# Soft-MoE expert outputs of a two-layer vision tower: stored from ScalarE's DMA queue instead of SyncE's, and read back in two sets

## What is computed

```python
xn = l2norm(x); phin = scale * l2norm(phi)
logits = einsum('bmd,dnp->bmnp', xn, phin)
d = softmax(logits, axis=1)                     # dispatch: over the tokens of an image
c = softmax(logits over n)                      # combine: over the 64 experts
xs = einsum('bmd,bmnp->bnpd', xn, d)            # one row for each image and expert
h = gelu(einsum('bnpd,ndh->bnph', xs, w1) + b1)
ys = einsum('bnph,nhd->bnpd', h, w2) + b2
y = einsum('bnpd,bmnp->bmd', ys, c)
```

## Time and profile before

| what | value |
|---|---|
| median of three runs | 980.36 us (977.6 to 984.06) |
| profiled execution, its own time | 982.76 us |
| its span, first to last instruction | 980.9 us |
| busy: TensorE, VectorE, ScalarE, GpSimd | 858.5, 455.5, 318.1, 280.1 us |
| experts stage with its combine | about 262 to 476 us of the span |
| bytes moved by DMA in all | 128.93 MB |

### The profile page before, as it was taken

How to read it: one execution, slowest core, us unless ns; L and a number is a source line. 1 busy time by engine, 2 the same in 40 slices (tenths; PEclk the granted TensorE clock), 3 DMA queues, 4 the chain that set the end, 5 groups by cost and what they waited for, 6 DMA issues and landing times. The chain is left out here.

```text
span 980.9 us, 17879 instructions
## 1 busy us (share of the span) xinstructions
PE 858.5 (88%) x6209; PEld 621.5 (63%) x6209; DVE 455.5 (46%) x1520; ACT 318.1 (32%) x904; POOL 280.1 (29%) x242
## 2 busy tenths in 40 slices
PE   6899999899999999893997999977465999999991
PEld 6787888676466655463854777757453666666661
DVE  6864565548443322241654688836781222222220
ACT  2544333237433332240042566633101121221210
POOL 1540000000000000000233455530027488888444
PEclk9999999799899999996997899985556999999996
DMA  8992000270089999982500000002005354455222
GB/s 265 281 329 97 2 2 2 81 305 2 23 320 423 423 422 423 425 263 70 175 1 1 1 2 0 1 2 53 24 24 140 79 105 104 92 101 104 39 24 25
DMA packets 59881, 128.93 MB, mean 131 GB/s; under 512 B 26334, under 2 KB 42256, under 8 KB 50112
## 3 DMA queue, kind: packets, MB, share of 16 engines
q1 hardware_dynamic: 29858, 118.61, 33.3%
q0 software_dynamic: 29952, 9.36, 7.0%
HBM read 115.76 MB, written 11.49 MB: 130 GB/s over the span
## 5 line engine op out<-in xcount | busy, mean ns | idle before, releaser
L1831 POOL DMA_INDIRECT out_dram<-yr,put x48 | 105.7, 2203 | 58.3 <-issue 35.4
L1286 POOL MEMSET xg<- 96x74 f32 x1 | 0.2, 157 | 406.9 <-PE bank L1259 406.9
L1818 POOL DMA_INDIRECT zr<-z_rows,take x48 | 66.6, 1388 | 84.6 <-issue 84.6
L1895 PE MATMUL bank<-zTa,w 128*128 128x372 f32 x256 | 90.0, 496 | 0.8 <-DVE zTb L1969 0.8
L1978 DVE TENSOR_TENSOR hT<-sg,bank 128x372 f32<-128x372 f32 x64 | 31.8, 538 | 107.5 <-ACT sg L1939 63.1
L1895 PEld LDWEIGHTS bank<-zTa,w 128*128 128x128 f32 x256 | 47.5, 194 | 38.2 <-ACT sg L1939 8.4
L1143 DVE COPY eh<-bank 128x384 f32<-128x384 f32 x32 | 17.8, 558 | 110.6 <-PE bank L1181 110.6
L1909 PE MATMUL bank<-w2r,hT 128*124 128x192 f32 x384 | 66.1, 329 | 0.8 <-DVE hT L1978 0.8
L1939 ACT ACTIVATE sg<-bank 128x372 f32<-128x372 f32 x64 | 27.3, 478 | 115.4 <-PE bank L1900 115.4
L1909 PEld LDWEIGHTS bank<-w2r,hT 128*124 128x124 f32 x384 | 61.9, 187 | 3.8 <-issue 3.8
L1327 POOL TENSOR_TENSOR nl<-nl,nr 111x1036 f32<-111x1036 f32 x22 | 42.1, 1914 | 61.7 <-DVE nr L1437 61.7
(11 more groups left out here) (298 smaller groups left out, 1798.4 us busy)
## 6 DMA issues: line engine op xcount, KB each, us to landing
w1l<-in_w_dram SPq DMA_DIRECT2D x20, 1152.0 KB, 16.3
w2l<-in_w_dram SPq DMA_DIRECT2D x20, 1152.0 KB, 16.9
w1s<-in_w_dram SPq DMA_DIRECT2D x12, 1152.0 KB, 15.5
w2s<-in_w_dram SPq DMA_DIRECT2D x12, 1152.0 KB, 15.1
w<-in_w_dram SPq DMA_DIRECT2D x8, 1024.0 KB, 8.0
xt<-in_x_dram SPq DMA_DIRECT2D x22, 336.0 KB, 8.0
xT<-in_xT_dram SPq DMA_DIRECT2D x22, 333.0 KB, 7.4
w2r<-in_w2r_dram SPq DMA_DIRECT2D x8, 384.0 KB, 4.1
```

The source lines that it names most:

```text
L1818: nc.gpsimd.indirect_dma_start(zr[b][:, j, :], None, z_rows, bass.IndirectOffsetOnAxis(ap=take[:, k:k + 1], axis=0), bounds_check=NROW - 1 ...
L1831: nc.gpsimd.indirect_dma_start(rows_out, bass.IndirectOffsetOnAxis(ap=put[:, k:k + 1], axis=0), yr[e % 2][:, j, :], None, bounds_check=OUT ...
L1895: nc.tensor.matmul(bank[to + 2 * part + half][:, 0:HS], w13[b][:, 0, at:at + 128], zTa[b][:, half * HS:(half + 1) * HS], start=True, stop= ...
```

## The change

The stores move from SP's loop into ScalarE's: right behind the copy of a pair's outputs, ScalarE waits for that copy to be complete and issues the two stores from its own DMA queue. All 32 pairs are stored to `ys`; the direct transfers and `places` are gone. SP's loop then holds weight loads alone; behind the last it waits for output of pair 27, loads b2, waits for the stores of pairs 24 to 27, and reads pairs 0 to 27 back in six transfers of 28 partitions; then it waits for the stores of pairs 28 to 31 and reads these back in six transfers of four partitions. TensorE's wait at the products is for b2 and the twelve read-backs alone.

```diff
-DIRECT = 27
+FIRST = 27
 def experts_sp(sp):
-    for s in range(NPAIR + RING):
+    for s in range(NPAIR):
         q = s % RING
...
         if s >= RING:
             sp.wait_ge(s_dy, s - RING + 1)
         sp.dma_start(w2s[q][:], ins["w2"][s]).then_inc(s_w2[q], 16)
-        p = s - RING
-        if p >= 0:
-            b = p % EOB
-            sp.wait_ge(s_do, p + 1)
...
-        if p == DIRECT:
+        if s == NPAIR - 1:
+            sp.wait_ge(s_dy, FIRST + 1)
             sp.dma_start(e2[NE:2 * NE, 0:T], ins["b2"].rearrange("n (t d) -> n t d", d=ED)).then_inc(s_el, 16)
...
+    for first, last in ((0, FIRST), (FIRST + 1, NPAIR - 1)):
+        for p in range(last + 1 - EOB, last + 1):
+            sp.wait_ge(s_eoo[p % EOB], rows_out_by(p))
+        for k in range(2):
+            read_back(sp, slice(k * NPAIR + first, k * NPAIR + last + 1))
+
+def read_back(sp, n):
+    for g in range(2):
+        to = slice(g * NE + n.start, g * NE + n.stop)
+        sp.dma_start(e1[to, 0:T - 1], ys_of[n, g * (T - 1):(g + 1) * (T - 1)]).then_inc(s_el, 16)
+    sp.dma_start(e2[n, 0:T], ys_of[n, 2 * (T - 1):B]).then_inc(s_el, 16)
...
     def output(p):
...
         nc.scalar.copy(eo[p % EOB][:], bank[6 + b][:, 0:ED]).then_inc(s_do, 1)
+        act.wait_ge(s_do, p + 1)
+        for e in range(2):
+            act.dma_start(ys_of[p + e * NPAIR], eo[p % EOB][e * B:(e + 1) * B]).then_inc(s_eoo[p % EOB], 16)
...
-    pe.wait_ge(s_el, 16 * (1 + 2 * GB))
-    for b in range(EOB):
-        pe.wait_ge(s_eoo[b], rows_out_by(NPAIR - EOB + b))
+    pe.wait_ge(s_el, 16 * (1 + 4 * GB))
```

More of the change, by code:

```diff
@@ L1059, in experts_sp @@
         def experts_sp(sp):
-            for s in range(NPAIR + RING):
+            for s in range(NPAIR):
                 q = s % RING
[L1062 to L1070, removed]
-                p = s - RING
-                if p >= 0:
-                    b = p % EOB
-                    sp.wait_ge(s_do, p + 1)
[L1075 to L1081, removed]
-                if p == DIRECT:
-                    sp.dma_start(e2[NE:2 * NE, 0:T], ins["b2"].rearrange("n (t d) -> n t d", d=ED)).then_inc(s_el, 16)
[L1084 to L1092, removed]
@@ L1094, in places @@
-        def places(n):
-            return ((e1[n:n + 1, 0:T - 1], 0, T - 1), (e1[NE + n:NE + n + 1, 0:T - 1], T - 1, 2 * (T - 1)), (e2[n:n + 1, 0:T], 2 * (T - 1), B))
+                if s == EARLY:
+                    sp.wait_ge(s_h, 2 * T)
+                if s >= RING:
+                    sp.wait_ge(s_dh, s - RING + 1)
+                sp.dma_start(w1s[q][:], ins["w1"][s]).then_inc(s_w1[q], 16)
+                if s >= RING:
+                    sp.wait_ge(s_dy, s - RING + 1)
+                sp.dma_start(w2s[q][:], ins["w2"][s]).then_inc(s_w2[q], 16)
@@ L1097, in rows_out_by @@
+        def read_back(sp, n):
[3 more added lines that the diff above has]
+            sp.dma_start(e2[n, 0:T], ys_of[n, 2 * (T - 1):B]).then_inc(s_el, 16)
         def rows_out_by(p):
-            return sum(16 * (2 if r < DIRECT else 2 * GB) for r in range(p % EOB, p + 1, EOB))
+            return 32 * (p // EOB + 1)
         def experts_act(act):
```

## The result

The changed kernel takes 987.16 us in the median of 20 runs (984.31 to 993.95), the kernel before 984.42 us in 20 runs beside it (977.6 to 987.67). The ratio is 1.0042, with a 95% interval of 1.0025 to 1.0058: 2.7 us or 0.25 to 0.58% slower, inside the 1% of no change and inside the range forecast; the forecast was 3.0 us slower. The profiled execution took 986.35 us (before 982.76).

What follows compares the result with a forecast made beforehand. Weights set the pace late in the experts stage, then the products wait for read-backs: 446.5 + 2.8 + 12.2 = 461.5 us against 458.53, 3.0 later, so 985.8 us profiled, 983.4 median; own range 979 to 987, wider range 973 to 991.

Steps and rivals of the forecast that it cites:

- T: Time when TensorE's first product after the experts can start: 458.53 us before the change, 461.5 forecast.
- Earlier weights: SP's weight loads in the experts stage, no longer behind store waits: net 0.6 us earlier, bounds 2.1 earlier and 0.5 later.
- Stores on ScalarE: Waits and two store issues a pair on ScalarE: 1.3 us a pair, hidden under its 2.52 us of idling.
- Rival C: ScalarE becomes the bound as its issues wait for SP's: 10 us slower, with the tail 994 us; chance 0.09.
- First set right behind b2, issued before 431: Read-back of pairs 0 to 27 follows b2, which ends at 431.2 us; takes 15.1 us, to 446.3.
- rival D: Stores wait behind all that is queued; first set starts no earlier than 434.3 us; 986.3 to 988.7 us; chance 0.15.
- When it can start: Second read-back set waits for pair 31's stores, which land with the first set's end, 446.5 us.
- Second set: Read-back of pairs 28 to 31, 0.39 MB in six four-partition transfers: 2.8 us issue and landing plus 12.2 us.
- slow end: Second read-back's six four-partition transfers one after another at 27 GB/s: 14.6 us.
- Sum: First product at 446.5 + 2.8 + 12.2 = 461.5 us, 3.0 later than 458.53; profiled execution 985.8, median 983.4.
- Rival A: The last stores land early, by 440.2 us; first product at 456.6 to 459.0, time 979.6 us; chance 0.25.
- B: Few partitions cost nothing: second read-back takes 2.2 us, first product 11.3 us earlier, time 969.1 us; chance 0.08.

Runs made afterwards that it cites:

- one_set: The changed kernel with one read-back set of 32 rows behind all stores in place of two sets; ratio 0.9993 to the kernel before.
- wide: The changed kernel with one read-back set behind all stores, two transfers in place of six, one over 128 partitions with outermost dimension 2; ratio 1.0324 to the kernel before.
- wide64: One read-back set behind all stores, three transfers of 64 rows in place of six of 32; ratio 0.9995 to the kernel before.
- first23: The changed kernel with the sets cut at pair 23 in place of 27, 24 pairs then 8; ratio 1.0033 to the kernel before.
- two_sets_q: Two sets (28 pairs, then 4) in a layout spread by pair, the first on 112 partitions, the second on 16; ratio 0.9941 to the kernel before.

## Why the prediction was right, and which terms were not

The class, the sign and the size came out: 3.0 us forecast, 2.7 measured in the median, T at 461.5 forecast and 461.18 measured. The mechanism is the one forecast, but that the size came so near is luck: two terms of the sum were off by 4 us in opposite directions. With the late start alone T would have been 465.2, with the short second set alone 457.5, 1.0 us earlier than before.

- *Earlier weights*, 0.6 us earlier: not there. w1 is now issued 0.37 us after w2 in place of 2.89, yet DMA moved 259 and 389 GB/s in the first 10 us against 277 and 385, and from the stage's first matmul (263.37 before, 263.40 after, by TensorE's timeline) to the last copy there are 173.2 us before and 173.4 after. In one execution of each kernel here it is 172.4 to 173.4 us with SP's stores (four kernels) and 172.5 to 174.8 with ScalarE's (ten). The step that failed is the 2.1 us of bytes "under what 421 would give", of which half was to come back: none that these executions show did. Why was not tried.
- *Stores on ScalarE*: right. 0.56 us in the median, 1.10 us for most pairs, and the hidden copy still waits 2.66 us for TensorE (2.52 in the earlier trace rows). Rival C falls: no issue took over 1.3 us. SP's long issues in the kernel before lay where its loads piled up: the stores' median was 0.59 us from 280 to 344 us, where loads landed within 19 us of their issue, and 1.43 from 345 to 410, where they took 18 to 24. That the queue was full then, as the prediction has it, is likely, but no row shows it.
- *First set right behind b2, issued before 431*: wrong, 432.57. The step that failed is that pair 27's stores "should have landed by 425 to 427": they were issued from 420.13 and landed 7.7 and 11.9 us after their issue, the last at 432.5, and SP, which waits for them, went on only at 432.57. Stores beside large transfers took 7.3 us in the median and up to 14.2. This is what rival D said of the stores. The line for pair 27's two:

```profile
DMA to landing us min/median/max: 7.7/9.8/11.9
```

  It cost little by itself, since b2 held DMA at 0.94 and 189 GB/s until 434.
- *When it can start*, 446.5: 450.16, 3.7 us late. The mechanism is the one forecast, and one_set shows it: 1.9 us for pair 31's stores without a first set ahead, 12.0 with one. The size was off because the first set began and ended later: b2 was to end at 431.2 and held DMA until 434.
- *Second set*, 2.8 + 12.2 us: 11.0. Data ran at 42 GB/s from 451.0, 0.9 us after the issue, to 460.4. The set is 24 packets of 16 KB, one for each row of its six transfers; the other 24 that the trace counts are tiny (DMA queues from 450.2 to 461 us):

```profile
DMA packets 48, 0.39 MB, mean 36 GB/s; under 512 B 24, under 2 KB 24, under 8 KB 24
```

  The slow end had put them one after another at 27 GB/s; together they ran at 42. The lower bound of 9.8 us ("upper partitions fully beside") was the right one for the transfers: four of the six go to partitions 28 to 31 and 60 to 63, 16 packets, and at the 0.6 us of wide's packets that is 9.6 us, against 9.4 measured. That the two groups share one way in is argued from wide64 and the section of the Trainium skill named there, not shown apart. A share of 0.21 over 9.4 us is 1.3 us a packet, twice that of wide, which fits; but by the same working first23's second set, with two such groups of 16 packets, would take 9.6 us, and took 12.2. So it is not the whole account. Of the 2.8 us for start and landing 1.7 were there, 0.9 before the data and 0.8 behind it.
- *Sum*: -0.3 us on T. The profiled execution is 3.6 us longer for 2.65 us of T, although the 44 products took 1.1 us less than in the earlier trace rows (16.0 us at a granted clock of 0.91, against 17.1 at 0.85). The other 2 us lie behind the combine; nothing there was changed, and the medians differ by 2.7.
- Rival A fell with the stores' 12.0 us, B with the 11.0 us of the second set. D had the late start nearly right (its sign was 433 or later, 432.57 measured) and was wrong on the time, since it took the same second set.

## What to carry to other kernels

Moving small stores to another engine's queue did not let them past large transfers here: they landed after 12 us from either queue and after 1.9 us with nothing ahead, so what has to be read back last should have nothing large issued before it. Before splitting a read-back so that most of it runs early, see whether it runs at full rate: here 3.1 MB at 220 GB/s became 428 GB/s by spreading the rows over all 128 partitions, 0.8% better than the kernel before, where cutting it at 28 pairs was 0.4% worse. Read the DMA share beside the GB/s: a share of 0.12 or 0.21 was too few rows in a transfer, full share at half the rate was a narrow target in one_set and wide64. That reading has an exception here: two_sets_q had nearly full share at half the rate on 112 partitions.

## What was not expected of the hardware

- A transfer of 128 rows whose outermost dimension was 2 ran on two of 16 engines: 54 GB/s at a share of 0.12, for 42 us, and made the kernel 3.2% slower.
- With all engines busy, 32 and 64 neighbouring partitions took 220 and 215 GB/s, 128 took 428.
- 56 rows over 112 partitions, in the layout in which 64 rows over 128 moved 428 GB/s, moved 200 at a share of 0.89.
